# Scores and weighted sums as split fp32r products in a three-block attention kernel

## What is computed

```
x = x + cross_attention(layernorm(x), ctx)   # 8 heads of 64, softmax over 257 context rows
x = x + gated_recurrence(layernorm(x))       # state = (1-w)*state + k v^T, out = r . state, 32 steps
x = x + low_rank_ffn(layernorm(x))           # gelu(x U1 V1 + b1) U2 V2 + b2
```

## Time and profile before

| | before |
|---|---|
| median of 3 runs | 1172.24 us (1168.86 to 1172.98) |
| profiled execution, its own time | 1169.72 us |
| its span, first to last instruction | 1167.6 us |
| granted TensorE clock, mean share of full speed | 0.983 |
| TensorE busy | 1113.0 us (95%) |
| VectorE busy | 617.7 us (53%) |
| ScalarE busy | 578.7 us (50%) |
| GpSimd busy | 256.2 us (22%) |

### The profile page before, as it was taken

How to read it: one execution, slowest core, us unless ns; L and a number is a source line. 1 busy time by engine, 2 the same in 40 slices (tenths; PEclk the granted TensorE clock), 3 DMA queues, 4 the chain that set the end, 5 groups by cost and what they waited for, 6 DMA issues and landing times.

```text
span 1167.6 us, 18934 instructions
## 1 busy us (share of the span) xinstructions
PE 1113.0 (95%) x7052; PEld 776.1 (66%) x7052; DVE 617.7 (53%) x1256; ACT 578.7 (50%) x1374; POOL 256.2 (22%) x324
## 2 busy tenths in 40 slices
...
DMA packets 57992, 79.06 MB, mean 68 GB/s; under 512 B 10288, under 2 KB 39728, under 8 KB 57904
## 3 DMA queue, kind: packets, MB, share of 16 engines
...
...
## 4 chain that ended last, share of the span: by engine, by line
PE 86%; DVE 5%; issue 4%; ACT 3%; POOL 2%; ACTq 1%; DVEq 0%; POOLq 0%
PE acc L357 9%; PE scores L334 9%; PE scores L337 7%; PE gb L423 7%; PE acc L359 6%; PE gb L309 5%; PE gb L395 5%; PE gb L446 5%; PE ptp L346 5%; PE gb L411 5%; PE gb L320 5%; PE gb L494 3%; PE gb L484 2%; PE gb L469 2%; PE gb L299 2%
## 5 line engine op out<-in xcount | busy, mean ns | idle before, releaser
L551 ACT ACTIVATE probs<-scores,nmax 128x257 f32<-128x257 f32 x256 | 119.4, 472 | 199.5 <-DVE nmax L682 199.4
L851 POOL TENSOR_TENSOR ptm<-probs,head 128x32 f32<-128x32 f32 x128 | 31.0, 242 | 657.6 <-DVE probs L689 657.6
L682 DVE TENSOR_REDUCE nmax<-scores 128x2 f32<-128x514 f32 x128 | 88.3, 690 | 156.2 <-PE scores L337 156.2
L741 DVE COPY_PREDICATED s<-mask,gb 128x256 f32<-128x256 uint8 x256 | 106.2, 442 | 89.9 <-PE gb L446 85.5
L357 PE MATMUL acc<-pt,raw_n 128*128 128x256 f32 x512 | 140.7, 397 | 0.0
L334 PE MATMUL scores<-raw_t,qk 128*128 128x257 f32 x512 | 132.6, 381 | 1.2 <-ACT qk L582 1.2
L561 ACT ACTIVATE pc<-acc 128x512 f32<-128x512 f32 x128 | 76.8, 600 | 112.4 <-PE acc L359 112.4
L357 PEld LDWEIGHTS acc<-pt,raw_n 128*128 128x128 f32 x512 | 89.9, 190 | 32.5 <-issue 22.3
L556 ACT ACTIVATE pt<-ptp 128x512 f32<-128x512 f32 x128 | 77.1, 602 | 51.7 <-PE ptp L346 50.1
L687 DVE RECIPROCAL rinv<-rsum 128x2 f32<-128x2 f32 x128 | 21.2, 166 | 144.0 <-ACT probs L551 143.9
L334 PEld LDWEIGHTS scores<-raw_t,qk 128*128 128x128 f32 x512 | 87.3, 190 | 8.5 <-issue 1.6
...
## 6 DMA issues: line engine op xcount, KB each, us to landing
raw_t<-in_ctx_t SPq DMA_DIRECT2D x128, 258.0 KB, 3.2
raw_n<-in_ctx_n SPq DMA_DIRECT2D x128, 192.0 KB, 2.4
...
vsp<-tail_values SPq DMA_DIRECT2D x256, 2.0 KB
...
```

The lines of the kernel that those rows point to most:

```text
L551: go(probs[n % 2][:, r, 0:L], scores[:, r, 0:L], ACT.Exp, bias=nmax[:, r:r + 1], accum_out=rsum[:, r:r + 1]).then_inc(s["exp_ready"], 1)
L682: v_.tensor_reduce(nmax[:], scores[:, :, 0:L], AX.X, ALU.max, negate=True)\
L741: last = v_.copy_predicated(s2[:, first:first + 3:2], mask[:, l0 + l:l0 + l + 1].to_broadcast([P, 2, P]), t[:, :, l * P:(l + 1) * P])
```

## The change

The scores and the weighted sums are computed in fp32r instead of float32. Each float32 operand is split into a high part (the value as written in fp32r) and a low part (value minus high part), and the product is the sum of high times high, low times high and high times low. For a batch there are five fp32r products of 258 columns for each of two row sets (before: two float32 products), and for the weighted sum ten of 256 columns (before four, two of them in half of the array). The 64 features of the second part stand twice in the 128 rows of `raw_t`; the folded query now holds the high part in rows 0 to 63 and the low part in rows 64 to 127, so one product covers both. All new products use the whole array.

The splits are new work. ScalarE writes the high parts of the transposed context (`t_hi`, 128x516), of the natural context (`n_hi`, 128x384) and, as before, the transposed probabilities (`pt_hi`). GpSimd writes the low parts of the context (`t_lo`, one instruction; `n_lo`, two). VectorE writes the low part of the transposed probabilities (`pt_lo`, 128x512) and, for each of the eight Qk tiles, two low parts (128x256 and 64x256), and now it is these that free the tile's bank. The rings of the context have two buffers; a buffer is reloaded when GpSimd has taken its low part. Three buffers are shared with others (`xt3`, `xn2`, `qf`). The tables `GAPS` and `STEPS` place VectorE's and GpSimd's work anew.

```diff
--- before
+++ after
@@ -25,7 +26,7 @@
-RING = 3
+RING = 2
@@ -75,7 +76,7 @@
-HAT_ORDER = ["k0", "r1", "k2", "r0", "r2", "k3", "r3"]
+HAT_ORDER = ["r1", "k0", "k2", "r0", "r2", "k3", "r3"]
@@ -134,9 +135,14 @@
-        pt = sb("pt", [P, LT, 256])
+        t_h, t_l = ([sb(f"{n}{i}", [P, 2, LP], F32R) for i in range(2)] for n in ("t_h", "t_l"))
+        nat = [sb(f"nat{i}", [P, LT, 2 * C], F32R) for i in range(2)]
+        pth, ptl = sb("pth", [P, LT, 256], F32R), sb("ptl", [P, LT, 256], F32R)
...
-        qk = [sb(f"qk{i}", [P, 2, G, 256]) for i in range(2)]
+        qk = [sb(f"qk{i}", [P, 2, G, 256], F32R) for i in range(2)]
+        qk_l = [sb(f"qk_l{i}", [P, G, 256], F32R) for i in range(2)]
@@ -144,6 +150,7 @@
+        xt3 = xt1
@@ -160,8 +167,9 @@
-        xn2, xt3 = sb("xn2", [P, 2, D]), sb("xt3", [P, 2, T])
-        pf, qf = sb("pf", [P, T]), sb("qf", [P, T])
+        xn2 = xn1
+        pf = sb("pf", [P, T])
+        qf = pf
@@ -210,12 +218,12 @@
-                    sp.wait_ge(s["scores_ready"], 2 * (n - RING + 1))
+                    sp.wait_ge(s["tlo_ready"], n - RING + 1)
...
-                    sp.wait_ge(s["acc_ready"], 2 * (n - RING + 1))
+                    sp.wait_ge(s["nlo_ready"], n - RING + 1)
@@ -324,23 +332,25 @@
-                pe.wait_ge(ctxt_in[n % RING], 16 * (n // RING + 1))
+                pe.wait_ge(s["tlo_ready"], n + 1)
...
-                x, w = raw_t[n % RING], qk[g % 2]
...
-                    mm(scores[:, r, 0:L], w[:, 0, b, r * P:(r + 1) * P], x[:, 0, 0:L], start=True, stop=False)
-                for r in range(2):
-                    half = slice(64 * r, 64 * r + 64)
-                    mm(scores[:, r, 0:L], w[half, 1, b, r * P:(r + 1) * P], x[half, 1, 0:L], start=False,
-                       stop=True).then_inc(s["scores_ready"], 1)
+                    r_ = slice(r * P, (r + 1) * P)
+                    w, w_l = qk[g % 2][:, :, b, r_], qk_l[g % 2][:, b, r_]
+                    h, l = t_h[n % 2], t_l[n % 2]
+                    terms = [(w[:, 0], h[:, 0]), (w_l, h[:, 0]), (w[:, 0], l[:, 0]), (w[:, 1], h[:, 1]),
+                             (w[:, 1], l[:, 1])]
+                    for k, (w_, x) in enumerate(terms):
+                        last = mm(scores[:, r, 0:LP], w_, x, start=k == 0, stop=k == len(terms) - 1)
+                    last.then_inc(s["scores_ready"], 1)
...
-                    pe.wait_ge(s["ptev_ready"], n)
+                    pe.wait_ge(s["ptl_ready"], n)
@@ -348,16 +358,18 @@
-                pe.wait_ge(s["ptev_ready"], n + 1)
-                pe.wait_ge(ctxn_in[n % RING], 16 * (n // RING + 1))
+                pe.wait_ge(s["ptl_ready"], n + 1)
+                pe.wait_ge(s["nlo_ready"], n + 1)
...
-                x = raw_n[n % RING]
+                x = nat[n % 2]
...
-                    mm(acc[:, 0], x[:, t, 0:P], pt[:, t], start=t == 0, stop=t == 1)
+                    for k, (c0, p_) in enumerate(((0, pth), (0, ptl), (2 * P, pth))):
+                        mm(acc[:, 0], x[:, t, c0:c0 + P], p_[:, t], start=t == k == 0, stop=t == 1 and k == 2)
...
-                    mm(acc[64 * t:64 * t + 64, 1], x[:, t, P:C], pt[:, t], start=True, stop=True)\
-                        .then_inc(s["acc_ready"], 1)
+                    for k, p_ in enumerate((pth, ptl)):
+                        last = mm(acc[:, 1], x[:, t, P:2 * P], p_[:, t], start=t == k == 0, stop=t == k == 1)
+                last.then_inc(s["acc_ready"], 1)
@@ -551,12 +563,24 @@
-            def pt_out(n):
+            def pt_hi(n):
...
-                go(pt[:], ptp[:], ACT.Copy).then_inc(s["ptev_ready"], 1)
+                go(pth[:], ptp[:], ACT.Copy).then_inc(s["pth_ready"], 1)
+            def t_hi(n):
+                act.wait_ge(ctxt_in[n % RING], 16 * (n // RING + 1))
+                if n > 1:
+                    act.wait_ge(s["scores_ready"], 2 * (n - 1))
+                go(t_h[n % 2][:], raw_t[n % RING][:], ACT.Copy).then_inc(s["thi_ready"], 1)
+            def n_hi(n):
+                act.wait_ge(ctxn_in[n % RING], 16 * (n // RING + 1))
+                if n > 1:
+                    act.wait_ge(s["acc_ready"], n - 1)
+                go(nat[n % 2][:, :, 0:C], raw_n[n % RING][:], ACT.Copy).then_inc(s["nhi_ready"], 1)
...
-                act.wait_ge(s["acc_ready"], 2 * n + 2)
+                act.wait_ge(s["acc_ready"], n + 1)
@@ -579,8 +603,8 @@
-                        drain(n, g, go(qk[g % 2][:, :, :, h * S:(h + 1) * S],
-                                       t[:].rearrange("p c (b s) -> p c b s", b=G), ACT.Copy))
+                        go(qk[g % 2][:, :, :, h * S:(h + 1) * S], t[:].rearrange("p c (b s) -> p c b s", b=G),
+                           ACT.Copy).then_inc(s["qkhi_ready"], 1)
@@ -626,8 +650,11 @@
-                        pt_out(n)
+                        pt_hi(n)
+                    if 0 <= n + 2 < B:
+                        t_hi(n + 2)
...
+                        n_hi(n + 1)
@@ -681,6 +708,10 @@
+            def pt_lo(n):
+                dve.wait_ge(s["pth_ready"], n + 1)
+                v_.tensor_tensor(ptl[:], ptp[:], pth[:].bitcast(F32), ALU.subtract).then_inc(s["ptl_ready"], 1)
@@ -716,6 +747,17 @@
+                elif n[:2] == "Qk":
+                    h = int(n[2])
+                    t = wait_tile(n, g)
+                    dve.wait_ge(s["qkhi_ready"], H * g + h + 1)
+                    h_ = slice(h * S, (h + 1) * S)
+                    of_batch = "p (b s) -> p b s"
+                    v_.tensor_tensor(qk_l[g % 2][:, :, h_], t[:, 0].rearrange(of_batch, b=G),
+                                     qk[g % 2][:, 0, :, h_].bitcast(F32), ALU.subtract)
+                    upper = qk[g % 2][64:128, 1, :, h_]
+                    drain(n, g, v_.tensor_tensor(upper, t[64:128, 1].rearrange(of_batch, b=G), upper.bitcast(F32),
+                                                 ALU.subtract))
@@ -798,10 +840,10 @@
-                    [[], [], ["f1-1", "f2-1", "f3-1", "i1-1", "i2-1"]],
-                    [["Y2-2"], ["xn2-2"], ["i3-1", "pw-1", "bw-1", "k1-1", "b1-1"]],
-                    [["ln0+2"], [], ["p1-1"]],
-                    [["xn0+2", "b2-1"], [], ["p2-1"]],
+                    [[], [], ["Qk0+1", "Qk1+1", "f1-1", "f2-1", "f3-1"]],
+                    [["Y2-2"], ["xn2-2"], ["Qk2+1", "Qk3+1", "i1-1", "i2-1", "i3-1", "pw-1"]],
+                    [["bw-1", "k1-1"], ["b1-1"], ["Qk4+1", "Qk5+1", "p1-1", "ln0+2"]],
+                    [["Qk6+1", "Qk7+1"], ["b2-1"], ["p2-1", "xn0+2"]],
@@ -827,6 +869,8 @@
+                    if 0 <= n < B:
+                        pt_lo(n)
@@ -851,6 +895,17 @@
+            def t_lo(n):
+                pool.wait_ge(s["thi_ready"], n + 1)
+                p_.tensor_tensor(t_l[n % 2][:], raw_t[n % RING][:], t_h[n % 2][:].bitcast(F32), ALU.subtract)\
+                    .then_inc(s["tlo_ready"], 1)
+            def n_lo(n):
+                pool.wait_ge(s["nhi_ready"], n + 1)
+                x, raw = nat[n % 2], raw_n[n % RING]
+                p_.tensor_tensor(x[:, :, 2 * P:3 * P], raw[:, :, 0:P], x[:, :, 0:P].bitcast(F32), ALU.subtract)
+                p_.tensor_tensor(x[:, :, C:2 * P], raw[:, :, P:C], x[:, :, P:C].bitcast(F32), ALU.subtract)                    .then_inc(s["nlo_ready"], 1)
@@ -877,6 +932,8 @@
+                if g == 0:
+                    pool.wait_ge(wb_in, W_B)
@@ -891,8 +948,8 @@
-            STEPS = [[[], []], [[], ["ln1-1"]], [[], []], [[], []], [["ln2-2"], ["k0-1", "xb+0"]],
-                     [["ln0+2"], ["r1-1", "k2-1", "r0-1"]], [[], ["r2-1", "k3-1"]], [[], ["r3-1", "ob-2"]]]
+            STEPS = [[[], []], [[], ["ln1-1"]], [[], []], [[], []], [["ln2-2"], ["xb+0"]],
+                     [[], ["r1-1", "k0-1", "k2-1", "r0-1", "ln0+2"]], [[], ["r2-1", "k3-1"]], [[], ["r3-1", "ob-2"]]]
@@ -910,11 +967,14 @@
-            pool.wait_ge(wb_in, W_B)
...
+                    if 0 <= n + 2 < B:
+                        t_lo(n + 2)
+                    if 0 <= n + 1 < B:
+                        n_lo(n + 1)
```

5 lines of the change are left out of this document (3 added, 2 removed).

## The result

The changed kernel takes 1241.4 us (median of 4 runs, 1240.4 to 1243.9) against 1172.1 for the kernel before on the same chip: ratio 1.061, 95% interval 1.058 to 1.064. The forecast was 1221, with 1115 to 1285.

What follows compares the result with a forecast made beforehand. TensorE bound every round before; afterwards VectorE binds rounds 5 and 6, a transfer round 7. A full stage +4.5: stages 1 to 12 +54, with the other parts +49, so 1169.7 becomes 1219, 1221 for the median; range 1115 to 1285.

Steps and rivals of the forecast that it cites:

- TensorE's part: TensorE alone would need 60.7 us per stage instead of 68.2; rounds 0 to 4 fall from 44.5 to 39.5.
- the 0.2 us per change between whole and half array: Attention products on TensorE: 22 changes per stage vanish at about 0.2 us each, saving 4.4 us.
- Rival (c): An fp32r product on TensorE costs 0.215 us, not 0.11: about 82 us per stage, 1390 in all; chance 0.06.
- Rival (b): TensorE stays the bound throughout: 16 x -7.5 + 3 gives 1055 us; chance 0.08.
- Rounds 5 to 7: VectorE's chain gives probabilities at 49.3 and 58.6 us; round 7's transfer chain, 14.1 us, ends the stage at 72.7.
- that bank: Round 5: Qk7 waits for Qk4's bank, which VectorE frees only behind the product; no time given.
- the lock of 0.5 in round 6: VectorE's product normalising the probabilities is blocked by GpSimd's context low parts; 0.5 us counted once, in round 6.
- Rival (a): Round 7's raw_t is there when ScalarE asks: round 7 8.5, stage 67.1, total 1148 (1150 for the median); chance 0.13.
- The 98 ns per product: TensorE's fp32r products at 256 columns, estimated between 81 and 131 ns; would take another 0.24 us off a round.
- rival d: Clock falls behind the waits in rounds 5 and 7: 1.3 to 3 us more per stage, 1240 to 1265; chance 0.14.
- Stage 0: First stage, taken as having no recurrence yet: -5 us.
- the block of 16 small issues: 16 small transfers, 9.4 us of SP's queue, ahead of a raw_t load: cost nothing, or 1 to 2 us if late.

Runs made afterwards that it cites:

- Experiment 4: The changed kernel with 8 fp32r products per batch instead of 20, all low terms left out of the sums, every split still made: 1210.3 us, ratio 1.033.
- experiment 5: High parts only: 8 fp32r products, no VectorE or GpSimd splits, with the tables, ring of three and issue order of the kernel before: 1060.3 us, ratio 0.908.
- experiment 1: The changed kernel with the load of x at b = 7 issued behind the two context loads of its round: 1198.5 us, ratio 1.023.
- experiment 2: The changed kernel without low parts of the folded query on VectorE; ScalarE's copy frees the Qk tile's bank: 1197.1 us, ratio 1.022.
- experiment 8: experiment 1 plus ln0 and xn0 moved to rounds 0 and 1 of the next stage, k1 and last Qk tile into VectorE's idle time: 1171.6 us, ratio 1.002.
- experiment 6: The changed kernel with extra overwritten products while TensorE waits, six in round 5 and five in round 7: 1242.2 us, ratio 1.060.
- Experiment 12: experiment 8 with bw and k1 moved to GpSimd, and the 16 small transfers issued in two halves, at b = 5 and b = 6: 1155.2 us, ratio 0.988.
- experiment 11: experiment 8 with bw and k1 on GpSimd behind round 5's tail column, and pw moved behind that round's row maximum: 1168.2 us.

## Why the prediction was right, and where its terms were off

**TensorE's part: right.** Rounds 0 to 4 were to fall to 39.5 and measure 40.65 in a stage at full clock. The shortfall per round, 0.17 to 0.28, is that of 20 products of 0.12 instead of 0.11 (0.2); the 0.2 us per change between whole and half array is therefore borne out to some hundredths. Experiment 4 shows the 0.12 by itself. Rival (c), 0.215, is refuted. Rival (b), TensorE the bound throughout, is refuted too: it is 87% busy, and experiment 5 shows that even with no low parts it would not be.

**Rounds 5 to 7: the chains came out on time, TensorE's part behind them did not.** The stage shown starts at 526.18. The probabilities of round 5 were forecast at 49.3 us of the stage and are there at 575.8, that is 49.6; those of round 6 at 58.6, measured 58.9 (585.1); the end at 72.7, measured 72.7. What is off is where the rounds are cut. The prediction ended round 5 when VectorE was done; the transposition comes 2.9 us later (578.69), because TensorE first runs Qk6's and Qk7's products, which wait for Qk4's bank until VectorE has taken its low parts (576.6) and then last 2.0 us at the low clock:

```profile
575.72 0.42 DVE L756 TENSOR_TENSOR qk_l<-gb,qk 128x256 fp32r<-128x256 f32 x1
576.15 0.43 DVE L759 TENSOR_TENSOR qk<-gb,qk 64x256 fp32r<-64x256 f32 x1
...
576.68 0.76 PE L328 MATMUL gb<-qs,wk 64*128 64x256 f32 x1 [1.62 <-issue]
...
578.69 1.11 PE L356 MATMUL ptp<-ident,probs 128*128 128x128 f32 x4
```

The prediction named that bank and gave it no time. So round 5 is 11.87 instead of 9.8, and round 6 gets it back: 8.15 instead of 9.3, as VectorE's chain runs on meanwhile. That the chain came out to 0.3 us is partly luck: its errors cancel. It starts 0.8 later than forecast (38.6 us into the stage, not 37.8), and each of its three Qk pairs was taken 0.43 too short (1.35, measured 1.78). Against that, k1 was taken too long (1.6, measured 1.02), and p1 too (1.6, measured 1.3); the wait of 0.3 ahead of the first pair and the lock of 0.5 in round 6 did not occur in this stage, whose norm product takes 0.70. Round 7 took 12.26 instead of 14.1 since the transposition that opens it is late too; from the probabilities to the end it is 13.8 against 14.1, of which the way to the landing is 7.2 against 8.1 and the rest 6.6 against 6.0. Experiments 1 and 2 confirm the two mechanisms with one change each. Rival (a), the transfer free, is what experiment 1 makes of round 7. It gives 1198 and not 1150, though the rival too had VectorE's chain in rounds 5 and 6: the stage is 69.9 and not 67.1 (rounds 0 to 4 by 1.2, 5 and 6 by 0.9, 7 by 0.8 longer), and stage 0 is 6.6 us longer than before where the rival had 5 less. The rival's own terms (14 x -1.1, -11, +3) add up to 1146 and not to 1148.

**Two rules.** The 98 ns per product that was estimated from the Trainium skill (TensorE: Matmul & The Clock Gate, Back-to-back issue gap) is not borne out here: 120 ns at 256 and 258 columns. The lock that the Trainium skill describes (SBUF — State Buffer, Who interferes with whom) agrees with this case's rows: VectorE's norm product takes 777 ns in the mean, 695 before; k1 takes 1.02 us beside GpSimd and 0.68 without (experiment 8).

**The clock (rival d): happened as well.** 1.6 us of scores at 0.21, round 0 at 9.82 instead of 9.21. Worth about 1 us per stage (experiment 6), so it accounts for most of what stages 1 to 12 cost (+5.5 each) over the forecast (+4.5). The forecast gave it 0.14 as a case of its own; it was no alternative to the forecast but came on top of it. That the measured 1241 lies in this rival's 1240 to 1265 is therefore no sign that the clock made the difference; the sum below shows what did.

**The sum: 25 us short between the profiled executions, 20 at the medians.** Stages 1 to 12 +65.6 against +54. **Stage 0 +7.8 against −5: the largest single error.** The prediction took the stage as one without recurrence; but its rounds are short, so the block of 16 small issues, costed at nothing, made ScalarE wait 5.34 us for `raw_t`:

```profile
61.63 9.48 SPq L250 DMA_DIRECT2D vsp<-tail_values  x16
71.16 0.44 SPq L222 DMA_DIRECT2D raw_t<-in_ctx_t  x1
...
73.98 0.63 ACT L574 ACTIVATE t_h<-raw_t 128x516 fp32r<-128x516 f32 x1 [5.34 <-DMA raw_t<-in_ctx_t]
```

VectorE's Qk parts stand in the same rounds. Experiment 12 removes just this wait, and experiment 1 takes 1.3 us from round 7 of this stage. The fill was +6.2 against +3. Stages 13 and 14 were +4.1 against +3, and stage 15 −0.1 against −6. Behind the last transposition the profile is 9.4 us shorter (82.1 against 91.4), where nothing was forecast. The length of this part goes with the clock: the mean granted clock is 0.88 in the change and 0.81 before, and in experiments 8 and 11, with the same work there, it measures 82.1 us at 0.88 and 88.8 at 0.81. Why the clock differs there from one profile to the next stays open. The change cannot claim these 9.4 us; without them the sum would be 35 us short.
